# Float16 pairs for the output product, its low parts on GpSimd, and new orders on every engine

## What is computed

```python
x = x + attn(layernorm(x), wq, wkv, wo)       # 32 heads, q and k of 128, v of 128, causal
x = x + ffn(layernorm(x), k0, k1, k2)         # three 512x512 products with weights +1 / -1
# attn: q, k, v = x @ wq, wkv ; probs = softmax(causal(q @ k.T * 192**-0.5))
#       attn = probs @ v ; return attn.reshape(S, 32 * 128) @ wo
```

## Time and profile before

| what | us |
|---|---|
| median of 3 runs (1137.81 to 1138.96) | 1138.8 |
| the profiled execution's own time | 1138.74 |
| its span, first to last instruction | 1136.9 |
| PE busy (96%) | 1092.0 |
| DVE busy (79%) | 895.9 |
| ACT busy (60%) | 678.0 |
| POOL busy (59%) | 667.6 |
| one steady pair | 65.65 |

### The profile page before, as it was taken

One profiled execution on the slowest core, in us unless ns is written; L12 is line 12 of the kernel. 1 busy time (PEld: TensorE's weight loads), 2 busy tenths in 40 slices (PEclk: granted clock), 3 DMA queues, 4 the chain that ended last, 5 costly groups with the idle time before them and its releaser, 6 DMA issues.

```text
span 1136.9 us, 18752 instructions
## 1 busy us (share of the span) xinstructions
PE 1092.0 (96%) x6223; PEld 655.2 (58%) x6223; DVE 895.9 (79%) x1797; ACT 678.0 (60%) x1334; POOL 667.6 (59%) x682
## 2 busy tenths in 40 slices
...
GB/s 157 88 99 84 119 108 128 100 116 94 96 112 109 121 114 114 82 117 109 91 121 114 124 82 119 112 76 121 117 130 89 117 107 81 118 93 115 92 1 75
DMA packets 367584, 118.25 MB, mean 104 GB/s; under 512 B 313088, under 2 KB 361344, under 8 KB 367488
## 3 DMA queue, kind: packets, MB, share of 16 engines
...
...
## 4 chain that ended last, share of the span: by engine, by line
PE 75%; DVE 12%; issue 6%; ACT 4%; POOL 3%; DMA 0%; SPq 0%; POOLq 0%; ACTq 0%; DVEq 0%
PE psC L1108 42%; PE psS L1108 16%; PE psC L1231 16%; DVE p L975 3%; DVE qk L907 2%; POOL wqk L487 2%; ACT raw L674 2%; POOL wqk L484 1%; DVE res L991 1%; DVE attn L958 1%; ACT attn L728 1%; DVE bound L930 1%; DVE psS L968 0%; DVE bound L936 0%; DVE bound L933 0%
## 5 line engine op out<-in xcount | busy, mean ns | idle before, releaser
L1108 PE MATMUL psC<-xb,wqk 128*128 128x512 f16 x1356 | 328.1, 381 | 12.5 <-POOL wqk L487 10.9
L706 ACT ACTIVATE psS<-psS,negmax 128x128 f32<-128x128 f32 (+7 forms) x256 | 182.8, 714 | 221.3 <-DVE negmax L968 220.4
L1108 PE MATMUL psC<-wos,attn 128*128 128x512 f32 x768 | 253.5, 441 | 13.5 <-DVE attn L958 10.1
L968 DVE CUSTOM_DVE_ANT_0 psS<-psS,mask,undo_qk 128x128 f32<-128x128 f32 (+7 forms) x256 | 208.4, 820 | 62.2 <-PE psS L1108 60.5
L975 DVE SCALAR_TENSOR_TENSOR p<-psS,p 128x128 f16<-128x128 f32 (+7 forms) x256 | 192.6, 752 | 60.2 <-ACT p L714 57.1
L1108 PE MATMUL psS<-qkT 128*128 128x512 f16 (+3 forms) x1152 | 230.0, 327 | 1.2 <-DVE p L975 0.7
L1108 PEld LDWEIGHTS psC<-xb,wqk 128*128 128x128 f16 x1356 | 124.5, 98 | 160.3 <-issue 36.3
L1231 PE MATMUL psC<-pT,v 128*128 128x512 f16 (+3 forms) x1152 | 197.8, 326 | 0.0
L991 DVE SCALAR_TENSOR_TENSOR res<-psC,rinv,res 128x512 f32<-128x512 f32 x256 | 190.1, 743 | 9.3 <-DVE rinv L982 8.1
L1108 PE MATMUL psC<-wvs,xb 128*128 128x256 f16 x1536 | 188.5, 273 | 0.4 <-POOL wvs L487 0.4
L484 POOL TENSOR_TENSOR wqk<-raw,one 128x512 f16<-128x512 f32 x122 | 115.9, 950 | 110.4 <-ACT raw L674 97.8
...
## 6 DMA issues: line engine op xcount, KB each, us to landing
...
pT<-p SPq DMA_TRANSPOSE x256, 4.3
wrow<-wmax_rows SPq DMA_DIRECT2D x45, 64.0 KB, 4.7
...
```

Source lines behind the costliest of these rows:

```text
L706: nc.scalar.activation(row, row, ACT.Exp, bias=negmax[:, n:n + 1], scale=-1.0, accum_out=rowsum[:, j % 2, n:n + 1]) \
L968: nc.vector.tensor_tensor_reduce(row, row, mask[:, S - width:S], undo_qk[:, j % 2:j % 2 + 1], 3e38, ALU.add, ALU.min, negmax[:, n:n + 1]). ...
L1108: last = nc.tensor.matmul(out_ap, w, x, start=k == 0, stop=k == len(terms) - 1)
```

## The change

The parts of `attn` and `wos` become float16. For this the output weights get the treatment of the value weights: a sum of squares per partition (`mx2`), a power of two (`sc2` in the opening; in the steady cycle `sc1` makes that of the values and that of the output weights together), and a scaling (`r2`), once for each pair of heads. The one put and get of a pair that carried the value weights' sums now carries both, as 128 x 2 numbers, and so waits for `mx2`. Both heads' output weights are loaded together, by `lo0@0`.

Behind `pv`, ACT copies the PSUM result to a float32 buffer (`keep_pv`), then writes the float16 high part from it (`attention_hi`, step ah), and POOL writes the low part (`attention_lo`, step al); DVE's `pv_lo` goes. The PSUM bank is free once the copy is made. The power of two is undone at the end, in `invert_sums`, by one more small DVE multiplication for each head. All five orders and the banks are new.

```diff
-    pv1@-1 s4@0 v0@0 s5@0 v1@0 x3@1 v2@0 s6@0 v3@0 x4@1 s7@0 x5@1 o4@-1 x6@1 o5@-1 x7@1 v4@0 o6@-1 x1@2 v5@0 s0@1
-    x2@2 o7@-1 s1@1 pv0@0 s2@1 v6@0 o0@0 s3@1 o1@0 v7@0 o2@0 s4@1 o3@0 s5@1 pv1@0 s6@1 x3@2 s7@1 o4@0 x4@2 o5@0 x5@2
-    x6@2 o6@0 x7@2 o7@0 pv0@1 x1@3 o0@1 s0@2 o1@1 s1@2 x2@3 o2@1 s2@2 o3@1 s3@2""", """
-    y0@2 spread1@2 y1@2 spread2@2 turn4@2 turn5@2 turn6@2 turn7@2 v0@2 v1@2 v2@2 s0@2 s1@2 y2@2 s2@2 s3@2 y3@2 v3@2
-    s4@2 v4@2 s5@2 y4@2 v5@2 s6@2 y5@2 s7@2 y6@2 v6@2 y7@2 v7@2""", "")
+    pv1@-1 s5@0 x3@1 x4@1 s6@0 x5@1 s7@0 x6@1 v0@0 o4@-1 x7@1 v1@0 o5@-1 v2@0 o6@-1 x1@2 v3@0 s0@1 x2@2 o7@-1 s1@1
+    pv0@0 v4@0 s2@1 v5@0 s3@1 v6@0 o0@0 v7@0 o1@0 s4@1 o2@0 s5@1 pv1@0 o3@0 s6@1 s7@1 o4@0 x3@2 o5@0 o6@0 x4@2 o7@0
+    x5@2 pv0@1 x6@2 x7@2 o0@1 x1@3 s0@2 s1@2 o1@1 o2@1 s2@2 x2@3 s3@2 o3@1 s4@2""", """
+    spread1@2 y0@2 y1@2 spread2@2 turn4@2 turn5@2 v0@2 turn6@2 turn7@2 v1@2 v2@2 s0@2 v3@2 s1@2 y2@2 s2@2 y3@2 s3@2
+    v4@2 v5@2 s4@2 y4@2 s5@2 y5@2 s6@2 s7@2 y6@2 y7@2 v6@2 v7@2""", "")
 
 SCALAR_ORDERS = ("""
-    r1@0 e6@-1 h6@-1 r0@1 e7@-1 h7@-1 qk2@0 pv0@-1 qk3@0 snap0@1 qk1@0 e0@0 h0@0 e1@0 h1@0 mx0@2 e2@0 h2@0 e3@0 h3@0
-    e4@0 v0@0 pv1@-1 h4@0 qk0@1 e5@0 v1@0 v2@0 h5@0 v3@0 e6@0 h6@0 e7@0 mx0@3 r0@2 h7@0 qk1@1 qk2@1 mx1@2 qk3@1 v4@0
-    v5@0 snap0@2 e0@1 h0@1 e1@1 h1@1 pv0@0 e2@1 v6@0 h2@1 e3@1 h3@1 v7@0 e4@1 h4@1 qk0@2 e5@1 h5@1 pv1@0""", """
-    nhi0@2 nhi1@2 nhi2@2 keep0@2 nhi3@2 mx0@3 keep1@2 keep2@2 mx1@2 keep3@2 root1@2 r1@2 vhi0@2 vhi1@2 nhi4@2 nhi5@2
-    y0@2 nhi6@2 keep4@2 keep5@2 nhi7@2 v0@2 keep6@2 y1@2 keep7@2 mx0@4 e0@2 h0@2 e1@2 h1@2 v1@2 v2@2 y2@2 e2@2 h2@2
-    e3@2 y3@2 r0@3 h3@2 part0@2 part1@2 e4@2 h4@2 v3@2 v4@2 e5@2 y4@2 h5@2 part2@2 part3@2 v5@2 y5@2 e6@2 h6@2 e7@2
-    h7@2 y6@2 r0@4 v6@2 y7@2 v7@2""", "")
+    e6@-1 h6@-1 e7@-1 h7@-1 r0@1 mx0@2 pv0@-1 ah0@-1 qk3@0 qk1@0 qk2@0 mx2@0 e0@0 h0@0 e1@0 snap0@1 h1@0 e2@0 h2@0
+    e3@0 h3@0 e4@0 h4@0 pv1@-1 qk0@1 r1@0 e5@0 h5@0 ah1@-1 r2@0 e6@0 h6@0 v0@0 qk1@1 r0@2 v1@0 qk2@1 e7@0 v2@0 h7@0
+    snap0@2 v3@0 e0@1 h0@1 qk3@1 mx0@3 e1@1 h1@1 v4@0 pv0@0 ah0@0 v5@0 e2@1 h2@1 qk0@2 e3@1 v6@0 h3@1 v7@0 mx1@2
+    e4@1 h4@1 e5@1 h5@1 pv1@0 ah1@0""", """
+    nhi0@2 nhi1@2 nhi2@2 nhi3@2 mx1@2 mx0@3 r1@2 y0@2 keep0@2 root1@2 vhi0@2 vhi1@2 keep1@2 keep2@2 nhi4@2 keep3@2
+    y1@2 nhi5@2 v0@2 keep4@2 nhi6@2 nhi7@2 keep5@2 v1@2 keep6@2 keep7@2 mx2@2 v2@2 e0@2 h0@2 r0@3 e1@2 v3@2 h1@2
+    part0@2 y2@2 e2@2 h2@2 mx0@4 y3@2 v4@2 e3@2 v5@2 h3@2 part1@2 e4@2 h4@2 e5@2 h5@2 r2@2 y4@2 part2@2 y5@2 part3@2
+    e6@2 e7@2 h6@2 y6@2 r0@4 v6@2 y7@2 v7@2 h7@2""", "")
 
 VECTOR_ORDERS = ("""
-    m0@0 o0@-1 m1@0 l0@0 o1@-1 l1@0 a2@1 o2@-1 m2@0 m3@0 l2@0 l3@0 o3@-1 m4@0 m5@0 pv1@-1 l4@0 a3@1 v0@0 v1@0 v2@0
-    l5@0 m6@0 rv0@0 a4@1 v3@0 m7@0 a5@1 l6@0 sc0@2 o4@-1 a6@1 a7@1 o5@-1 l7@0 v4@0 o6@-1 v5@0 m0@1 l0@1 a2@2 m1@1
-    o7@-1 l1@1 pv0@0 m2@1 o0@0 m3@1 l2@1 o1@0 v6@0 l3@1 v7@0 m4@1 o2@0 m5@1 sc1@2 l4@1 o3@0 l5@1 pv1@0 m6@1 a3@2
-    m7@1 o4@0 sc0@3 l6@1 a4@2 o5@0 a5@2 a6@2 a7@2 o6@0 l7@1 pv0@1 o7@0""", """
-    nlo0@2 nlo1@2 nlo2@2 nlo3@2 stat4@2 stat5@2 stat6@2 stat7@2 scale1@2 sc1@2 rest1@2 apply4@2 apply5@2 apply6@2
-    apply7@2 nlo4@2 nlo5@2 sc0@3 nlo6@2 y0@2 nlo7@2 y1@2 v0@2 m0@2 m1@2 l0@2 sum0@2 l1@2 sum1@2 m2@2 m3@2 v1@2 l2@2
-    y2@2 v2@2 y3@2 sum2@2 l3@2 m4@2 part0@2 m5@2 l4@2 v3@2 sum3@2 v4@2 l5@2 m6@2 y4@2 part1@2 m7@2 v5@2 l6@2 sc0@4
-    y5@2 part2@2 l7@2 v6@2 y6@2 v7@2 part3@2 y7@2""", "")
+    a5@0 a6@0 a7@0 l7@-1 o0@-1 m0@0 m1@0 l0@0 o1@-1 m2@0 l1@0 l2@0 m3@0 o2@-1 m4@0 o3@-1 a2@1 l3@0 sc1@0 m5@0 l4@0
+    a3@1 a4@1 l5@0 m6@0 a5@1 m7@0 sc0@2 a6@1 o4@-1 a7@1 v0@0 l6@0 v1@0 o5@-1 o6@-1 v2@0 l7@0 rv0@0 m0@1 v3@0 l0@1
+    a2@2 m1@1 l1@1 v4@0 o7@-1 m2@1 v5@0 m3@1 l2@1 o0@0 v6@0 l3@1 v7@0 m4@1 m5@1 o1@0 o2@0 l4@1 l5@1 o3@0 m6@1 m7@1
+    o4@0 a3@2 o5@0 o6@0 sc0@3 l6@1 a4@2 o7@0""", """
+    nlo0@2 nlo1@2 nlo2@2 nlo3@2 stat4@2 stat5@2 sc1@2 stat6@2 stat7@2 scale1@2 y0@2 rest1@2 apply4@2 apply5@2 sc0@3
+    apply6@2 nlo4@2 apply7@2 nlo5@2 y1@2 nlo6@2 v0@2 nlo7@2 v1@2 sum0@2 m0@2 sum1@2 m1@2 l0@2 sum2@2 v2@2 m2@2 l1@2
+    v3@2 sum3@2 y2@2 m3@2 l2@2 y3@2 v4@2 sc2@2 l3@2 m4@2 v5@2 part0@2 m5@2 l4@2 part1@2 l5@2 m6@2 y4@2 m7@2 y5@2
+    part2@2 sc0@4 part3@2 l6@2 v6@2 y6@2 v7@2 y7@2 l7@2""", "")
 
 SYNC_ORDERS = ("""
-    put1@0 put0@1 t0@-1 get1@0 t1@-1 get0@1 t2@-1 t3@-1 lo0@-1 t4@-1 t5@-1 t6@-1 lqk0@2 t7@-1 t0@0 put0@2 t1@0 t2@0
-    get0@2 t3@0 t4@0 lqk0@3 t5@0 lv0@2 t6@0 lo0@0 t7@0""", """
-    lqk0@4 lo0@2 put0@4 t0@2 t1@2 get0@4 t2@2 t3@2 t4@2""", "")
+    lv0@0 t0@-1 put0@1 t1@-1 t2@-1 t3@-1 get0@1 t4@-1 lqk0@2 t5@-1 lo0@0 t6@-1 put0@2 put1@0 t7@-1 get0@2 get1@0
+    t0@0 t1@0 t2@0 t3@0 t4@0 t5@0 lqk0@3 t6@0 t7@0""", """
+    lo0@2 lqk0@4 put1@2 t0@2 get1@2 t1@2 t2@2 put0@4 t3@2 t4@2 get0@4""", "")
 
 POOL_ORDERS = ("""
-    sum0@1 qk0@1 wv2@0 wqk0@2 qk2@1 qk1@1 qk3@1 wo0@0 sum0@2 wv0@2 wv1@2 qk0@2 wqk0@3 wo0@1 qk2@2 qk1@2 qk3@2""", """
+    qk0@0 wo0@-1 wqk0@1 al0@-1 qk2@0 qk1@0 qk3@0 sum0@1 qk0@1 wv0@0 wv1@0 al1@-1 wqk0@2 qk1@1 qk2@1 wv2@0 wo0@0
+    al0@0 qk3@1 sum0@2 al1@0""", """
     wqk0@2 wk0@2 wv0@2 wv1@2 wqk0@3 wk0@3""", "")
 
...
-BANKS = "301230123012301201230120123012301230123012"
+BANKS = "301230123012301230123012012301230123012012"
...
-    if h == 0 and (step[0] in ("mx", "sc", "r", "put", "get", "lqk", "lv") or step[0] == "wv" and step[2] == 2):
+    if h == 0 and (step[0] in ("lqk", "lv") or step[0] in ("mx", "sc", "r", "put", "get") and step[2] == 0 or step[0] == "wv" and step[2] == 2):
...
-        return [x for x in steady if exists(g, x)]
+        late = [("pv", -1, 1), ("ah", -1, 1)] + [("o", -1, t) for t in range(4, 8)]
+        return [x for x in steady if exists(g, x) and x not in late] + [x for x in late if x in steady]
...
-        attn = sb("attn", [P, 2, CH], F32R)
+        attn = sb("attn", [P, 2, CH], F16)
+        attn32 = sb("attn32", [P, 2, CH], F32)
...
-        raw = sb("raw", [P, 7, 512], F32)
+        raw = sb("raw", [P, 8, 512], F32)
...
-        wos = sb("wos", [P, 2, D], F32R)
+        wos = sb("wos", [P, 2, D], F16)
...
+        wrow_pair = sb("wrow_pair", [P, P, 2], F32)
...
+        undo_o = sb("undo_o", [P, 1], F32)
+        wmax_dram = nc.dram_tensor("wmax_rows", (2, P), F32).ap()
+        wpair_dram = nc.dram_tensor("wmax_pair", (P, 2), F32).ap()
...
-        def load_out(q, h):
-            q.dma_start(raw[:, 4, :], wo_v[:, bass.ds(h, 1), :].rearrange("p a d -> p (a d)")) \
-                .then_inc(loaded["o"], 16)
+        def load_out(q, pair):
+            for k in range(GH):
+                q.dma_start(raw[:, 6 + k, :], wo_v[:, bass.ds(pair * GH + k, 1), :].rearrange("p a d -> p (a d)")) \
+                    .then_inc(loaded["o"], 16)
...
 
-            at = 2 if n else j % 2
-            (wait_pair if n else wait)(q, rows_max[n], g, 1, j, 1)
-            q.dma_start(wmax_dram[at:at + 1, :].rearrange("a p -> p a"), wmax[:, at:at + 1]) \
-                .then_inc(rows_out[n], 16)
+            if n:
+                wait_pair(q, rows_max[1], g, 1, j, 1)
+                q.sem_inc(turn_go, 1)
+                wait_pair(q, rows_max[2], g, 1, j, 1)
+                q.dma_start(wpair_dram, wmax[:, 2:4]).then_inc(rows_out[1], 16)
+            else:
+                wait(q, rows_max[0], g, 1, j, 1)
+                q.dma_start(wmax_dram[j % 2:j % 2 + 1, :].rearrange("a p -> p a"), wmax[:, j % 2:j % 2 + 1])                     .then_inc(rows_out[0], 16)
 
         def rows_from_dram(q, g, j, n):
 
-            at = 2 if n else j % 2
-            (wait_pair if n else wait)(q, rows_out[n], g, 16, j, 0 if n else -16)
-            q.dma_start(wrow[:, at, :], wmax_dram[at, :].partition_broadcast(P)).then_inc(rows_in[n], 16)
-
+            if n:
+                wait_pair(q, rows_out[1], g, 16, j, 16)
+                q.dma_start(wrow_pair[:, :, :].rearrange("p r a -> p (r a)"),
+                            wpair_dram.rearrange("r a -> (r a)").partition_broadcast(P)).then_inc(rows_in[1], 16)
+            else:
+                wait(q, rows_out[0], g, 16, j, -16)
+                q.dma_start(wrow[:, j % 2, :], wmax_dram[j % 2, :].partition_broadcast(P)).then_inc(rows_in[0], 16)
...
             elif step == "lo":
-                wait(q, wo_lo, g, 1, j, 0)
-                load_out(q, g * GH + j)
+                wait_pair(q, wo_lo, g, 2, j, 0)
+                load_out(q, g + j // GH)
...
-                wait(pool, loaded["o"], g, 16, j, 16)
+                wait_pair(pool, scaled[2], g, 1, j, 1)
                 wait(pool, done["o"], g, 8, j, 0)
-                nc.gpsimd.tensor_tensor(wos[:, HI, :], raw[:, 4, :], one[:, :].to_broadcast([P, D]), ALU.mult) \
-                    .then_inc(wo_hi, 1)
-                wait(pool, wo_hi, g, 1, j, 1)
-                nc.gpsimd.tensor_tensor(wos[:, LO, :], raw[:, 4, :], wos[:, HI, :].bitcast(F32), ALU.subtract) \
-                    .then_inc(wo_lo, 1)
```

(45 more changed lines are left out.)

67 lines of the change are left out of this document (36 added, 31 removed).

## The result

The changed kernel takes 1170.89 us (median of 4 runs, 1167.79 to 1175.18), the kernel before 1138.30 (1137.41 to 1138.96): 1.0289 times as long, 95% interval 1.0247 to 1.0332. That the kernel would be slower was forecast; by how much was not: 1145 was predicted, and the time lies above the range.

A forecast was written before the change was run, and what follows sets the result against it. PE was taken to bound the kernel, its float16 gain spent waiting for the put. From 1138.7 us, steady pairs added 2.3, opening 2.0 and end 2.0: 1145.0, own range 1138 to 1152, stated range 1106 to 1160.

The forecast's parts named there:

- The gain of float16: On PE, float16 o chains take 0.65 us each, removing 0.8 to 1.2 us per pair, 12 to 18 over 15 pairs.
- The base of 62.3 us: A steady pair's matmuls on PE, all float16 and none waiting, take 62.3 us of the real 65.65.
- The path: Through put1@0, get1@0, t0@0, h4@0, l5@0, s7@0 comes 3.3 us late, at X + 21.1, counted from X, the end of x7@2.
- t7@-1 was priced at 7.0 us: Transpose behind put1@0 in SP's queue lands with the put at about X + 10, making pv1@-1 2.4 us late.
- P: Time from put1@0's issue to get1@0's, taken as 7.3 us; below 7.15 the changed kernel wins.
- rival A: The put (put1@0) is quick or not missed, so the kernel gets faster: 1106 to 1126 us, middle 1112; chance 0.38.
- B: Rival: put takes the 9 us of two at once, or POOL and ACT add a wait: 1163 to 1170; chance 0.12.
- opening and end: Opening's extra put, get and sc2@2 before l3@2 cost 2.0 us; bare hand-overs at the end cost another 2.0.
- this term of 3.5 us: PE's waits in a steady pair: 3.3 us through the put, plus 0.15 added, rounded to 3.5.
- the short waits that the prediction gave 0.9: Three at the cycle's start, al0@-1, s0@2 for qk2's low part, x2 for `snap`: together 0.9 us, within the 3.3.
- rival A's floor of 63.2: With a quick put, the steady period is not under 62.3 + 0.9 = 63.2 us.
- The bare hand-over from pv to o: For the last head it grows from 1.5 to 2.6 us; two such add 2.0, bounds 0 and 3.3.

The follow-up runs named there:

- run 1: The kernel before with only the types of attn and wos changed to float16, without the power of two for the output weights: 1122.55 us.
- run 2: The changed kernel with the pair's put and get run only for the first pair, whose sums every later pair reuses: 1151.29 us.
- run 6: The changed kernel with each head's put writing 8 bytes per partition instead of 4, its get reading 128 KB, three `squares` slots: 1116.09 us.
- run 9: All puts 8 bytes wide in the old orders: in the kernel before 1140.17 us, in that kernel with float16 attn and wos 1125.23 us.

## Why the prediction was right and wrong

**The gain of float16: right.** An o chain takes 0.65 in the timeline of the changed kernel, and a steady pair of run 1 is 1.00 us shorter (0.8 to 1.2 forecast). The base of 62.3 us for a pair without waits holds as well, see below.

**The path: right in its steps, not in its prices.** put, get, t0@0, h4@0, l5@0 and s7@0 follow each other as forecast. In the pair shown x7@2 ends at X = 566.8 (start to start); get1@0 goes at X + 9.5 (9.9 forecast) and t0@0 at X + 10.1 (10.3), but t0@0 lands at X + 16.4 (15.4), since it takes 6.3 us and not 5.1, and s7@0 begins at X + 22.0 (21.1). h4@0 stands waiting for t0@0 in all 14 pairs, 1.6 to 5.6 us. t7@-1 was priced at 7.0 us by one row; it lands after 5.9 to 10.2, in the mean 8.2. The mean wait of pv1@-1, 1.9 us, still falls into the forecast 1.5 to 2.4. That is luck, since PE comes to pv1@-1 late too, in the pair shown at X + 9.4 instead of 7.6.

**Which put: wrong.** The prediction put its price P on put1@0 and named rival A "the put is quick". The pair's put, 8 bytes wide, is quick where no 4-byte put goes ahead of it: in the opening its get goes 4.1 us behind it (33.34 to 37.43), where 7.2 was taken. In the pairs get1@0 goes 5.0 to 10.0 us behind put1@0, in the middle 7.2, for another reason than P: in 11 of them it stands only behind get0@2, and this behind the put of 4 bytes; in three it waits for its own put, up to 2.7. (One of the three is the last pair, where no put0@2 goes ahead, and it is the 5.0.) That 7.2 meets the 7.3 of the forecast is luck. The prediction had both in the earlier trace rows and noted that put0@2 goes 3 us ahead, but took it for finished with put1@0's. It also overlooked that lo0@0's wait for POOL holds put0@2 back. So the half of A that speaks of the new put came true and gained nothing. B, at a chance of 0.12, rightly guessed that put0@2 adds to the time, and its 1163 to 1170 lies near the result; but it took two puts together for the cause, where the get goes 8.4 behind put0@2 alone in run 2, and the clock is not in it. One sum of A is off too: at P = 7.15 the periods are equal, but with the 4.0 us of opening and end the times are equal at P = 6.9.

**The sum.** The steady pair was to take 62.3 + 3.5 = 65.8 us; it took 67.8. The failed step is this term of 3.5 us for the time that PE loses in a pair: it measured 5.5. By PE's own time the 2.0 that it left out are the clock, 1.1, and the short waits, 0.9:

- The clock's fall, 1.1 us a pair. The prediction let a wait cost its own length. Here a wait of 2.85 us was followed by 2.85 lost in the chain behind it, and in the seven such pairs pv1@-1 lost 1.4 to 2.9. But part of this takes the place of a forecast wait: in these seven pairs PE has no wait at s6@0 and s7@0, in five of the other seven it has 0.6 to 2.3. From the start of pv1@-1 to that of v0@0 the seven take 14.9 us in the mean and the others 14.0, against 12.8 in run 6. So what the clock alone adds is not shown; it is less than 1.1 a pair if the waits would otherwise have stood there.
- Waits, 67.8 - 62.3 - 1.1 = 4.4, against 3.5. Of the 4.4, 3.4 are in the waits view. What most of the rest is, the timeline of PE in the kernel of run 6 shows, from x6@2 to pv1@-1:

```profile
602.05 2.75 PE L1138 MATMUL psC<-xb,wqk 128*128 128x512 f16 x12
605.21 0.81 PE L1138 MATMUL psC<-wos,attn 128*128 128x512 f16 x3 [0.41 <-POOL attn L565]
605.86 1.46 PE L1138 MATMUL psC<-xb,wqk 128*128 128x512 f16 x6
607.53 0.66 PE L1138 MATMUL psS<-qkT 128*128 128x128 f16 x6 [0.21 <-issue]
...
614.03 4.38 PE L1261 MATMUL psC<-pT,v 128*128 128x512 f16 x24
```

From 602.05 to 614.03 it is 11.98 us. The chains in it, at the prediction's prices, make 42 x 0.2157 + 3 x 0.163 + 3 x 0.109 + 6 x 0.056 = 10.2, and 1.8 are waits, where the view lists 0.41, 0.21 and, at s2, 0.33 in brackets. A listed wait begins at the modelled end of a matmul, 0.16 us after the next could have begun (a record of 0.38 against 0.22 from start to start), which makes these three 1.4; the other 0.3 are in two pauses that are not listed, behind s2 and ahead of s4. In run 6 a pair takes 64.14, 1.84 above 62.3. So the base is right, and the short waits that the prediction gave 0.9 cost 1.8. The third of them was to be x2 behind `snap`; it is s2@2 behind its low part. That also makes rival A's floor of 63.2 too low by 0.9.

So 14 pairs, each 2.03 longer than forecast, make 28.4 us. Against that, opening and end were forecast at 2.0 each, and a fifteenth pair at 0.15; they took 1.0, -0.2 and -2.0, which is 5.4 less. (In run 1 the last pair is 1.25 shorter than before; the types alone give that much.) The bare hand-over from pv to o before the last pv1 is indeed longer, 2.67 us of waiting against 2.31, but that is all. 1145.0 + 28.4 - 5.4 = 1168.0, the profiled time.

**What the change is worth, split up** (medians of different series): types in the old orders -15.5 us (run 1); the wide form of the puts in them +2.7 (run 9); new orders and paths with a put that lands quickly, 1116.1 against 1125.2 for run 9's float16 kernel, a further -9; the 4-byte put side by side in these orders +54.8. Of these 54.8, the 14 pairs hold (67.82 - 64.14) x 14 = 51.5.

**Open.** Why 512 bytes side by side land late is not settled: the runs tell spacing from size and count the same packets, but how such a put is spread over the DMA engines, or how DRAM takes the writes, was not tried. Whether a wait is followed by the low clock isn't told by its length alone: at pv1@-1 waits of 1.8, 2.6, 2.85, 3.2, 3.25, 3.4 and 3.9 us were, those of 2.0 and 2.2 were not.
